# Five steps of the next layer between the last MLP products, and the attention's last steps issued together with the first MLP steps

## The reference

```python
def attn_layer(x, Wqkv, qs, ksc, Wo):        # 16 heads of 64 channels
    q, k, v = split_heads(x @ Wqkv)
    q = l2norm(q) * qs;  k = l2norm(k) * ksc
    q = q * cos * scale + rotate_half(q) * sin * scale
    k = k * cos * inv + rotate_half(k) * sin * inv
    return local_attention(q, k, v) @ Wo      # softmax over a band of 32 tokens
def ffn_layer(x, g, bln, W1, b1, W2, b2):     # 341 hidden channels
    xn = (x - mu) / sqrt(var + 1e-05) * g + bln
    a, gate = split(xn @ W1 + b1)
    return a * gelu(gate) @ W2 + b2
```

## Time and profile before

| | us |
|---|---|
| median of 3 runs | 4446.3 (4444.8 to 4446.31) |
| profiled execution | 4449.5 |
| its span, first to last instruction | 4447.7 |
| mean granted clock of PE | 0.967 |
| one layer (1325.01 to 1948.19) | 623.2 |

### The profile page before, as it was taken

The page is one execution under the profiler, slowest core; times in us unless marked ns, Lnnn a source line. Parts: engine busy times, 40 slices in busy tenths (PEclk is TensorE's granted clock), DMA queues, the critical chain, the costliest instruction groups (busy, mean ns, idle before and its releaser), DMA issues.

```text
span 4447.7 us, 138701 instructions
## 1 busy us (share of the span) xinstructions
PE 3986.8 (90%) x49504; PEld 3146.8 (71%) x49504; DVE 3672.2 (83%) x8896; ACT 3560.3 (80%) x11591; POOL 3379.8 (76%) x2461
## 2 busy tenths in 40 slices
PE   7998885999979999889999889999899998899997
PEld 5666664777767777667777667777677776677776
DVE  7998887888868888778888778888688887788886
ACT  6888984888948888748888568888388887588884
POOL 4544447999939999759999579998499996699993
PEclk9999997999999999989999989999899999899999
DMA  3000000000010000010000000000100000000001
GB/s 80 0 0 1 0 0 15 5 0 0 1 39 4 2 0 0 7 33 3 2 0 0 20 21 5 0 0 2 37 4 2 0 0 12 14 6 0 0 0 34
DMA packets 81158, 39.29 MB, mean 9 GB/s; under 512 B 60085, under 2 KB 73267, under 8 KB 80947
## 3 DMA queue, kind: packets, MB, share of 16 engines
q1 hardware_dynamic: 80946, 36.56, 3.2%
HBM read 21.92 MB, written 2.10 MB: 5 GB/s over the span
## 4 chain that ended last, share of the span: by engine, by line
DVE 34%; PE 28%; ACT 22%; issue 12%; POOL 2%; DVEq 1%; DMA 0%; SPq 0%; ACTq 0%; POOLq 0%
ACT pair L966 13%; PE bank L749 6%; PE bank L679 6%; DVE top L1360 5%; DVE prob L1378 5%; PE bank L672 5%; DVE by_cos L1328 5%; ACT prob_t L983 4%; DVE norm L1343 4%; PE pair L823 4%; PE bank L771 4%; DVE by_sin L1336 3%; DVE top L1286 3%; DVE qk_parts L1261 2%; DVE ctx_all L1427 2%
## 5 line engine op out<-in xcount | busy, mean ns | idle before, releaser
L1081 POOL TENSOR_TENSOR rnorm<-norm2g,neg_half 128x16 f32<-128x16 f32 x384 | 1115.5, 2905 | 237.0 <-DVE norm2g L1353 236.5
L1073 POOL TENSOR_TENSOR rotated<-by_cos,by_sin 128x512 f32<-128x512 f32 x768 | 980.8, 1277 | 178.7 <-DVE by_sin L1336 175.1
L966 ACT ACTIVATE pair<-pair,top 128x128 f32<-128x128 f32 x3072 | 1044.0, 340 | 84.7 <-DVE top L1360 51.1
L1093 POOL TENSOR_TENSOR rotated<-rotated,rnorm 128x512 f32<-128x512 f32 x768 | 784.9, 1043 | 0.5
L1328 DVE TENSOR_TENSOR by_cos<-bank,rot_cos 128x512 f32<-128x512 f32 x768 | 531.2, 692 | 276.1 <-PE bank L679 274.1
L679 PE MATMUL bank<-wqkv_high,xt_high 128*128 128x512 f32 (+1 forms) x1536 | 663.1, 432 | 34.1 <-ACT squares L957 34.1
L749 PE MATMUL bank<-prob_t,vout 128*32 128x128 f32 x12288 | 499.2, 280 | 201.8 <-ACT prob_t L983 181.7
L977 ACT ACTIVATE vout<-bank 128x512 f32<-128x512 f32 (+1 forms) x810 | 465.5, 575 | 238.6 <-PE bank L749 230.6
L966 ACT ACTIVATION_READ_ACCUMULATOR pair<-pair,top 128x1 f32 x3072 | 628.6, 205 | 0.0
L1378 DVE TENSOR_TENSOR prob<-pair,rsum 128x512 f32<-128x512 f32 x768 | 531.1, 692 | 41.1
L957 ACT ACTIVATE squares<-bank 128x512 f32<-128x512 f32 x768 | 466.1, 607 | 107.9 <-DVE by_sin L1336 96.0
(11 more groups left out here) (144 smaller groups left out, 8637.8 us busy)
## 6 DMA issues: line engine op xcount, KB each, us to landing
wqkv_sb<-in_L_ffn_Wqkv_dram SPq DMA_DIRECT2D x36, 256.0 KB, 4.1
ctx_all<-y SPq DMA_DIRECT2D x48, 128.0 KB
ctx_all<-y SPq DMA_DIRECT2D x48, 127.0 KB
wo_sb<-in_L_ffn_Wo_dram SPq DMA_DIRECT2D x48, 64.0 KB, 2.1
out_dram<-y SPq DMA_DIRECT2D x8, 256.0 KB, 3.5
w_sb<-in_L_ffn_W_dram SPq DMA_DIRECT2D x6, 341.0 KB, 3.1
w_sb<-in_L_ffn_W_dram SPq DMA_DIRECT2D x12, 64.0 KB
cst<-in_constants_dram SPq DMA_DIRECT2D x1, 582.0 KB, 3.5
```

What stands on the lines that cost most here:

```text
L966: last = nc.scalar.activation(at, at, ACT.Exp, bias=top[jl % 2][:, h:h + 1], accum_out=psum_raw[jl % 2][:, h:h + 1])
L1073: nc.gpsimd.tensor_tensor(rotated[j % 4][:, :, :, :], by_cos[j % 2][:, :, :, :], by_sin[j % 2][:, :, :, :], ALU.add).then_inc(c_rot, 1)
L1081: nc.gpsimd.tensor_tensor(rnorm[slot][:, :, :].rearrange("t g n -> t (g n)"), norm2g[slot][:, :, :].rearrange("t g n -> t (g n)"), neg_hal ...
L1093: nc.gpsimd.tensor_tensor(at, at, rnorm[slot][:, i, :].unsqueeze(2).to_broadcast([P, 2 * HG, DH]), ALU.mult).then_inc(c_unit, 1)
```

## The change

The arithmetic is the same. What is moved:

- The first five steps (`FILL`) of the next layer are issued on all engines between the last MLP pieces; `windowed` begins with step 5. Five layers are a loop, the sixth is unrolled (`layers`). A loop turn begins with step 5. The first two inputs get places of their own in bank 7 (`first_ps`), and their waits change.
- The down product has one bank (`mlp_out_ps`) instead of two and waits for `mlp_take` of the quad before.
- The hidden products move from the buffers of cosine and sine to `qk_t` and `vout[4:6]`, which frees those of the first steps.
- The emptying is written out for each engine (`drain`), with pieces of the MLP steps at other places. The last three turned heads go to bank 0 instead of bank 3.
- In every DVE step `win_max` stands ahead of `win_norms`. In `mlp_step` on DVE `mlp_take` stands between the hidden products.
- POOL splits the chunks of layer 0 ahead of its wait for the second attention. ACT has an Exp of one element ahead of the next layer's step 2.

```diff
-MLP_EARLY = (1, 3, 5, 7)
+ENDED = GROUPS // STEPS
+FILL = 5
...
-        hidden = [flat(b) for b in by_cos + by_sin + rotated[0:2]]
+        hidden = qk_t + vout[4:6]
...
-        out_ps = (bank[7], bank[6])
+        mlp_out_ps = bank[6]
+        first_ps = bank[7]
...
+        def layers(eng, first, body):
+
+            first()
+            with eng.Fori(0, DEPTH - 1) as layer:
+                body(layer, False)
+            body(DEPTH - 1, True)
...
@@ tensor engine @@
-                    if has(it * 2 + j - 5):
-
-                        pe.wait_ge(s_y_done, m - 1 + NQ)
+                    if has(it * 2 + j - 4):
+
+                        pe.wait_ge(s_f_b2, m)
...
+            def drain(layer):
+                for j in range(WIN_DRAIN):
+                    win_turn_probs(layer, ENDED, j)
+                    win_mask(layer, ENDED, j)
+                    win_scores(layer, ENDED, j)
+                    if j == 3:
+                        mlp_turn(layer, 0, 1)
+                    if j == 6:
+                        mlp_up(layer, 1, 0)
+                    win_sum_values(layer, ENDED, j)
+                    win_heads(layer, ENDED, j)
+                    win_project_out(layer, ENDED, j)
+                    if j == 4:
+                        mlp_turn(layer, 1, 0)
+                    if j == 6:
+                        mlp_turn(layer, 1, 1)
+                        mlp_up(layer, 1, 1)
+                mlp_down(layer, 1, 1)
+
+            def second_inputs(layer):
+                pe.wait_ge(s_y_done, (layer + 1) * NQ)
+                win_turn_next(layer, 0, 3)
...
+            def body(layer, last):
+                windowed(pe, win_step, layer)
+                drain(layer)
+                middle(pe, mlp_step, layer)
+                if not last:
+                    pe.wait_ge(c_vout, (layer + 1) * VOUTS)
+                    begin(layer + 1)
+                mlp_turn(layer, 4, 0)
+                mlp_up(layer, 4, 0)
+                if not last:
+                    pe.wait_ge(s_f_xt, (layer + 1) * NQ)
+                    win_products(layer + 1, 0, 0)
+                mlp_down(layer, 4, 0)
+                if not last:
+                    win_products(layer + 1, 0, 1)
+                mlp_up(layer, 4, 1)
+                if not last:
+                    win_products(layer + 1, 0, 2)
+                mlp_down(layer, 4, 1)
+                if not last:
+                    win_products(layer + 1, 0, 3)
+                mlp_down(layer, 5, 0)
+                if not last:
+                    win_products(layer + 1, 0, 4)
+                    second_inputs(layer + 1)
...
@@ scalar engine @@
+            def drain(layer):
+                for j in range(WIN_DRAIN):
+                    win_exponentials(layer, ENDED, j)
+                    if j:
+                        win_copy_values(layer, ENDED, j - 1)
+                        win_copy_heads(layer, ENDED, j - 1)
+                    if j == 4:
+                        mlp_copy(layer, 0, 1)
+                    win_copy_probs(layer, ENDED, j)
+                    if j == 5:
+                        mlp_copy(layer, 1, 0)
+                    if j == 6:
+                        mlp_gelu(layer, 1, 0)
+                        mlp_copy(layer, 1, 1)
+                        mlp_gelu(layer, 1, 1)
...
+                if not last:
+                    begin(layer + 1)
+                mlp_copy(layer, 4, 0)
+                mlp_gelu(layer, 4, 0)
+                if not last:
+                    win_copies(layer + 1, 0, 0)
+                    win_copies(layer + 1, 0, 1)
+                mlp_gelu(layer, 4, 1)
+                if not last:
+                    nc.scalar.activation(exp_of_one[:, :], one[:, :], ACT.Exp)
+                    for j in range(2, FILL):
+                        win_copies(layer + 1, 0, j)
+                    win_copy_next(layer + 1, 0, 3)
...
@@ gpsimd @@
+            def drain(layer, last):
+                win_unit(layer, ENDED, 0)
+                mlp_rstd(layer, 0, 0)
+                mlp_rstd(layer, 0, 1)
+                split_w1(layer)
+                if not last:
+                    pool.wait_ge(c_vproj, (layer + 1) * GROUPS)
+                    pool.wait_ge(c_sin, (layer + 1) * GROUPS)
+                    set_sines(layer + 1)
+                mlp_rstd(layer, 1, 0)
+                mlp_low(layer, 0, 1)
+                mlp_low(layer, 1, 0)
+                mlp_rstd(layer, 1, 1)
...
             for phase in (A, B):
                 prepare(phase, 0, 0)
                 attention(pool, step, phase)
+            for c in range(CHUNKS):
+                split_chunk(0, c)
             pool.wait_ge(s_added, 2 * NB)
             for b in shifted:
                 pool.memset(b[0:1, :, DH:P], 0.0).then_inc(s_zero_row, 1)
-            for c in range(CHUNKS):
-                split_chunk(0, c)
...
@@ vector engine @@
                 win_scale(layer, it, j)
+                win_max(layer, it, j)
                 win_norms(layer, it, j)
-                win_max(layer, it, j)
                 win_clamp(layer, it, j)
...
+            def mlp_step(layer, it, j):
+                mlp_stats(layer, it, j)
+                mlp_hidden(layer, it, j, 0)
+                mlp_take(layer, it, j)
+                mlp_hidden(layer, it, j, 1)
+                mlp_hidden(layer, it, j, 2)
+                mlp_normalise(layer, it, j)
+                mlp_bias(layer, it, j)
+
+            def drain(layer):
+                for j in range(WIN_DRAIN):
+                    win_recip(layer, ENDED, j)
+                    win_scale(layer, ENDED, j)
+                    win_max(layer, ENDED, j)
+                    win_add(layer, ENDED, j)
+                    if j == 0:
+                        mlp_stats(layer, 0, 0)
+                    if j == 1:
+                        mlp_normalise(layer, 0, 0)
+                    if j == 2:
+                        mlp_stats(layer, 0, 1)
+                    if j == 3:
+                        mlp_normalise(layer, 0, 1)
+                    if j == 4:
+                        mlp_stats(layer, 1, 0)
+                    if j == 5:
+                        mlp_normalise(layer, 1, 0)
+                        for k in range(3):
+                            mlp_hidden(layer, 1, 0, k)
+                        mlp_stats(layer, 1, 1)
+                    if j == 6:
+                        for k in range(3):
+                            mlp_hidden(layer, 1, 1, k)
+                    if j == 7:
+                        mlp_normalise(layer, 1, 1)
...
+            def finish_into(layer, after):
+                toks(after)
+                mlp_take(layer, 4, 0)
+                splits(after)
+                mlp_hidden(layer, 4, 0, 0)
+                mlp_bias(layer, 4, 0)
+                mlp_hidden(layer, 4, 0, 1)
+                mlp_hidden(layer, 4, 0, 2)
+                win_rotations(after, 0)
+                win_squares(after, 0)
+                mlp_take(layer, 4, 1)
+                win_rotations(after, 1)
+                mlp_hidden(layer, 4, 1, 0)
+                win_squares(after, 1)
+                win_tok_next(after, 0, 1)
+                mlp_hidden(layer, 4, 1, 1)
+                mlp_bias(layer, 4, 1)
+                mlp_hidden(layer, 4, 1, 2)
+                win_rotations(after, 2)
+                win_squares(after, 2)
+                mlp_take(layer, 5, 0)
+                win_rotations(after, 3)
+                mlp_bias(layer, 5, 0)
+                win_squares(after, 3)
+                mlp_take(layer, 5, 1)
+                win_rotations(after, 4)
+                mlp_bias(layer, 5, 1)
+                win_squares(after, 4)
+                win_split_next(after, 0, 3)
```

More of the change, by code:

```diff
@@ L666, in win_heads @@
                     pe.wait_ge(c_unit, g + 1)
-                    if has(it * STEPS + j - WIN.turn - 1) and not here(it, j, WIN.probs):
+                    if ended(it) and j == 0:
+                        pe.wait_ge(c_sq, (layer + 1) * GROUPS)
+                    if has(it * STEPS + j - WIN.turn - 1) and (ended(it) or not here(it, j, WIN.probs)):
                         pe.wait_ge(c_qk, g)
@@ L856, in _ @@
+            layers(pe, first, body)
         @block.scalar
@@ L1143, in set_sines, with first, body @@
                                             now[:, :, swapped].unsqueeze(2).to_broadcast([P, 2, HG, HALF]), ALU.mult).then_inc(c_sines, 1)
[L1145 to L1150 removed]
+            def first():
+                for j in range(FILL):
+                    win_step(0, 0, j)
+            def body(layer, last):
+                windowed(pool, win_step, layer)
+                drain(layer, last)
+                middle(pool, lambda layer, it, j: mlp_step(layer, it, j, last), layer)
+                mlp_low(layer, 4, 0)
+                if not last:
+                    for j in range(FILL):
+                        win_step(layer + 1, 0, j)
             for phase in (A, B):
@@ L1165, in _ @@
             set_sines(0)
```

(36 more changed lines are left out.)

219 lines of the change are left out of this document (122 added, 97 removed).

## The result

| | before | after |
|---|---|---|
| median of the runs (four each), us | 4446.1 | **4239.6** (4238.9 to 4241.3) |
| ratio, 95% interval | | 0.9537, [0.952, 0.9553] |
| profiled execution, us | 4449.5 | 4239.9 |
| its span, us | 4447.7 | 4238.0 |
| mean granted clock of PE | 0.967 | 0.986 |

The changed kernel is 206.5 us faster, 4.6%. The forecast was 192 us (4254, range 4205 to 4345): right, and 14 us short.

The account below looks back on a forecast made before the run. It took handshakes between four engines, none the bound by itself, as the limit. Loop 70, emptying 54, layer change 58 and prologue 10 sum to 192 us: 4449.5 less 192 is 4257.5, median 3.2 lower, 4254 us, range 4205 to 4345.

Parts of the forecast that it names:

- Loop: Attention loop: top ahead of the norm on DVE shortens DVE's ring, 0.8 us per eight steps, 70 us in all.
- ACT's ring of 3.81 us: Attention loop: exponentials, prob_t, value product, vout, qk_t; next to bound once DVE's ring falls from 3.895 to 3.6 us.
- Emptying: End of each layer's attention: reordered MLP pieces bring the last normed from +79.1 to +69.4; 9 us a layer, 54 us.
- The shift's transfer: Emptying: named as what is late next, 9.9 us from issue; statistics of the third quad come at +17.8.
- Layer change: Last normed to sixth projection, five changes: 32.4 us instead of 43.6, 11 us at four, 14 at the last, 58 us.
- the chain: Layer change: PE's hand-laid sequence from the last normed to the second inputs at 29.2 us, before the jump.
- step 3: Layer change: waits 0.7 us for square 2 and 0.6 for POOL's unit, done at 23.1 us.
- step 4: Layer change: the last of the first steps before the jump, done at 27.4 us, behind a down product at 25.8.
- Table loads: ACT at the layer change: two per layer, cost taken as 0; four more would cost 26 us in all.
- rival (b): Ends of layers give half, through extra table loads or waits missed in hand-laid chains: 4310 us, 15%.
- mlp_take: Middle loop on DVE: standing between hidden products ahead of normed, it loses 0.3 us on four steps together.
- Prologue: Before the layers: POOL's chunk splitting moved into its idle time, powers at 671.0 instead of 681.41, 10 us once.

Follow-up runs that it names:

- b_unrolled: The kernel before with its six layers written out on all four engines, no jump between layers: 4422.7 us, ratio 0.9951 to before.
- a_unrolled: The changed kernel with all six layers written out, so that no engine jumps back between layers: 4214.1 us.
- the added instructions: Three copies of the changed kernel, each attention step with an extra ACT Copy, DVE reciprocal or repeated PE mask products: 4294.7, 4236.7 and 4248.4 us.
- a_serial: The changed kernel with the next layer's five first steps issued behind the last MLP product instead of between the MLP products: 4288.8 us.

## Why the prediction was right, point by point

- **Loop: right in mechanism, short in size.** Forecast 70 us, 83.7 in the ledger, 92 for the swap alone. The step that failed is the last of its sum: worked out were 0.9 us per eight steps, and 0.8 was taken because "PE's own work is 31.0 of 32.7". PE at 97.7% takes 0.6 us more almost without a delay, so there was nothing to hold back for. Measured were 0.95 in the windows above (32.70 to 31.75) and 0.99 in the mean of all turns. Its split was right: from start to start of the exponentials, mean of six layers, the four plain steps fall from between 3.83 and 3.96 us to 3.81, 0.35 together (forecast 0.3), the two behind a token transpose from 4.21 and 4.04 to 3.81, 0.63 (0.6), and the two with the transpose stay at 4.60 and 4.31 (none). In after:

```profile
1706.69 0.34 ACT L1053 ACTIVATE pair<-pair,top 128x128 f32<-128x128 f32 x1
...
1711.00 0.34 ACT L1053 ACTIVATE pair<-pair,top 128x128 f32<-128x128 f32 x1
...
1714.81 0.34 ACT L1053 ACTIVATE pair<-pair,top 128x128 f32<-128x128 f32 x1
```

  Too few steps were counted as well: 122 lie between the landmarks, 15.25 times eight, not 14.6. Between `b_unrolled` and `a_unrolled`, which have no jumps, the loop's column falls by 89.7 (2972.9 to 2883.2), 0.98 x 15.25 x 6. In before and after it is 6 less, since the tail of four jumps costs 10.8 us there (2894.0 - 2883.2) and that of five jumps 4.9 before (2977.8 - 2972.9). The new bound was named rightly: ACT's ring of 3.81 us, by the added instructions.
- **Emptying: right.** 55.5 for 54. From the timeline of layer 1, counted from the first exponentials (1788.96): the sixth exponentials start at +18.0 (1806.99; laid out +17.8), first up product +21.9 (+21.8), third +37.1 (+36.5), last `normed` ends at +69.5 (+69.4):

```profile
1810.88 0.48 PE L849 MATMUL pair<-normed_high,w_high 128*128 128x512 f32 x1
...
1826.01 0.48 PE L849 MATMUL pair<-normed_high,w_high 128*128 128x512 f32 x1
...
1835.31 0.87 DVE L1590 BATCH_NORM_STATS2 stats<-ctx_all 128x6 f32<-128x128 f32 x4 [2.21 <-DMA ctx_all<-y]
...
1855.92 2.54 DVE L1605 TENSOR_SCALAR ctx_all<-ctx_all,mv,rstd 128x128 f32<-128x128 f32 x4
```

  The shift's transfer is what comes late next, as said: it is waited for 2.21 us in one step and 0.38 and 1.54 in two others. The prediction gave `normed` 1.4 us, and 2.2 beside `split_w1`; what POOL's chunks cost it in the later steps (2.54 where 1.10 is possible) was missed, and hidden in the sum because the same was true before.
- **Layer change: right in the sum, by two errors that cancel.** 60.9 for 58: 44.4 at the four jumps for 44, 16.4 at the last boundary for 14. From the last `normed` to the sixth projection 32.7 us (1858.46 to 1891.12) for 32.4. But the chain was 2.1 us shorter (second inputs at +27.1, not +29.2) and the jump longer, 5.13 on PE and 5.31 on DVE where 3.2 was kept from the earlier trace rows. POOL, counted as run dry, still works for 1.84 of the 5.31 us. That the two meet at 32.7 is luck. Of the 2.1 us some 1.1 are slips of the sum: the terms named for step 3 (0.7, 0.6 and 1.1 behind 20.1) give 22.5 and not 23.1, and step 4 is given 1.6 where a step's projection is 1.1. `a_serial` has the old gap still, about (2.83). The last boundary has no jump to make good the shorter chain: its sixth projection starts 27.4 us behind `normed` (3657.57, behind 3630.13), where 29.2 was forecast. Behind the jump PE's clock is at its lower level (0.50 in the window above), where the prediction had the higher one throughout. PE's timeline at a jump, then at the last boundary:

```profile
1885.55 0.32 PE L673 MATMUL bank<-cst,tok 128*64 128x128 f32 x1 [1.26 <-DVE y L1571]
...
1891.12 0.79 PE L699 MATMUL bank<-wqkv_high,xt_high 128*128 128x512 f32 x1 [5.13 <-issue]
...
3657.57 0.50 PE L699 MATMUL bank<-wqkv_high,xt_high 128*128 128x512 f32 x1
```

- **Table loads: right**, two per layer, none for Copy or Square between the Gelus. So rival (b) is out: no further loads, and the ends of the layers gave 116 us where it had half of 112. **`mlp_take`: right that it costs little, without knowing why it may not stand elsewhere** (75 us).
- **Prologue: right.** 10.5 for 10; the powers start at 671.01 (forecast 671.0), and DVE's wait for them, 11.76 in the earlier trace rows, is 1.60. POOL and DVE at that place:

```profile
671.01 2.02 POOL L1323 TENSOR_TENSOR rstd<-var,neg_half 128x4 f32<-128x4 f32 x2
...
672.14 2.14 DVE L1739 TENSOR_SCALAR y<-x,mv,rstd  x8 [1.60 <-POOL rstd L1323]
```

The parts taken singly come to 92 (swap) + 51 (emptying) + 49 (interleaving) + 10.5 (prologue, from the trace; not run alone) = 203 of 206.5 us, so they hardly touch each other. The 4 us left may be the unrolled last boundary, which no run took back alone; nor was any of the moved buffers undone.

## What to carry to other kernels

Look for the ring that closes latest, instruction start to instruction start over two steps, and not for the busiest engine: an engine at 98% took more work nearly for nothing, and one at 92% passed on 0.09 us in full in six of eight steps. When two users of a buffer become one, the place of the instruction that frees it decides (75 us here), and a stage that is faster in the one turn which lacks some side work shows what that work costs (24 us here). Putting work into an engine's waits can pay twice for PE, once for the wait and once for the granted clock (0.52 to 1.00 here). A loop's jump was worth unrolling in both kernels here, where all engines cross it together.

## What the runs showed of the hardware

- A backward jump of all engines cost 4.3 us in the kernel before, where they had run dry, and 6.4 in the changed one. Of these 3.15 to 3.5 and 4.9 to 5.3 us show as a gap ahead of DVE's first instruction; the rest lies in the steps behind it, in the changed kernel partly at the lower clock (0.50 from 1891.12 to 1895.00).
- A Copy of one element on ACT lasts 0.19 us and delays the next instruction by 0.09.
- DVE's SBUF-to-SBUF `normed` (four instructions) takes 1.10 us alone, 2.52 beside POOL's split of a chunk and 3.55 beside that of `w1`; single instructions of it end 0.08 to 0.09 us behind POOL's.
- ACT loads a table in 1.28 us. In the loop without the one-element Exp the load stands at the first ACT instruction of a turn, a Square, in all five turns.
